# Unrolled attention pipeline: key products one tile early, new slots for every step, joined narrow maxima, expert weights loaded into the front's buffers

## The reference, cut to what matters

```python
x = x + layernorm(L0_attn(layernorm(x)))     # x: 8 x 1024 x 256
x = x + layernorm(L0_ffn(layernorm(x)))

# L0_attn, per position, 16 heads of 16:
Q, K, V = rms(x, g1) @ Wq.T, rms(x, g1) @ Wk.T, rms(x, g1) @ Wv.T
kv1[e,d] = sum_h elu(K)[h,e] * V[h,d] * SCALE     # e in the first half of a head, kv2: in the second
attn[h,d] = sum_e elu(Q)[h,e] * kv1[e,d] - lmb * (the same with kv2)
attn = rms(head norm(attn), g3) + head norm(attn)
out = gelu(attn @ W1) @ W2.T + attn

# L0_ffn: causal softmax attention (16 query heads, 4 key heads, rotary), then 8 experts, 2 per token:
h = clip(residual + softmax(q k^T / 4, causal) v @ Wo)
o = (silu(f @ Wg[e]) * (f @ Wu[e])) @ Wd[e]     # f = rmsnorm(h), for the two chosen e
out = clip(h + sum of the two, weighted)
```

## Time and profile before

| | |
|---|---|
| median of 3 runs | 4241.21 us (4240.19 to 4244.3) |
| profiled execution | 4237.51 us, its span 4235.6 us |
| busy in the span | PE 3146.7, DVE 2483.6, POOL 1651.6, ACT 1599.7 us |
| mean granted TensorE clock | 0.843 |
| front | to about 3304 us; experts' matmuls about 3350 to 4143 us; the rest is the last layer norm |

### The profile page before, as it was taken

The page is one execution under the profiler, slowest core; times in us unless marked ns, Lnnn a source line. Parts: engine busy times, 40 slices in busy tenths (PEclk is TensorE's granted clock), DMA queues, the critical chain, the costliest instruction groups (busy, mean ns, idle before and its releaser), DMA issues. The chain is left out here.

```text
span 4235.6 us, 54665 instructions
## 1 busy us (share of the span) xinstructions
PE 3146.7 (74%) x17668; PEld 1857.1 (44%) x17669; DVE 2483.6 (59%) x5036; ACT 1599.7 (38%) x3644; POOL 1651.6 (39%) x2045
## 2 busy tenths in 40 slices
PE   3555777777767776777777677767887399999991
PEld 2433434443443444444434444443433266666660
DVE  4667776776677667767776776676563122222225
ACT  1222445444534443443345444435544122222223
POOL 4564433543553354345435443541312122222222
PEclk7677888788888888887888888888888699999995
DMA  1000000000000000000000000000000533333335
GB/s 36 3 9 7 7 9 9 10 19 7 22 14 14 14 15 21 9 19 9 20 7 20 16 13 13 14 17 6 21 16 30 161 61 55 55 60 56 55 52 164
DMA packets 102336, 123.25 MB, mean 29 GB/s; under 512 B 14048, under 2 KB 89824, under 8 KB 102112
## 3 DMA queue, kind: packets, MB, share of 16 engines
q1 hardware_dynamic: 76384, 85.54, 6.7%
q0 software_dynamic: 25728, 34.88, 4.8%
HBM read 58.23 MB, written 61.36 MB: 28 GB/s over the span
## 5 line engine op out<-in xcount | busy, mean ns | idle before, releaser
L752 ACT ACTIVATE PR<-SP_ 128x512 f32<-128x512 f32 (+3 forms) x1536 | 728.0, 490 | 1528.6 <-PE SP_ L1366 1019.0
L1042 DVE TENSOR_REDUCE NM<-MX 128x1 f32<-128x512 f32 (+3 forms) x1536 | 817.1, 551 | 657.3 <-PE MX L1322 398.2
L1319 PE MATMUL MX<-KST,QST 96*128 96x512 bf16 (+3 forms) x1536 | 540.6, 362 | 407.3 <-DVE NM L1042 353.9
L472 POOL TENSOR_TENSOR P<-QK,VS 128x2048 f32<-128x2048 f32 x128 | 478.8, 3740 | 860.8 <-DVE QK L863 860.8
L1363 PE MATMUL SP_<-QST,KST 99*128 99x512 bf16 (+3 forms) x1536 | 544.0, 357 | 67.4 <-ACT PR L752 53.7
L1319 PEld LDWEIGHTS MX<-KST,QST 96*128 96x128 bf16 x1536 | 155.8, 102 | 770.5 <-DVE NM L1042 560.4
L1646 POOL DMA_INDIRECT scratch_h<-Y,XG x136 | 211.6, 1556 | 632.4 <-DVE Y L1709 538.8
L1214 PE MATMUL SUM<-ident,P 128*128 128x128 f32 x2048 | 313.0, 319 | 138.1 <-POOL P L472 83.5
L1687 DVE TENSOR_TENSOR AG<-UB,SL 128x512 f32<-128x512 f32 x136 | 94.0, 691 | 488.5 <-PE UB L1726 488.5
L1380 PE MATMUL OA<-PR,V 128*32 128x512 f32 (+3 forms) x3072 | 354.4, 536 | 0.8 <-ACT PR L752 0.6
L1214 PEld LDWEIGHTS SUM<-ident,P 128*128 128x128 f32 x2048 | 285.3, 168 | 158.3 <-issue 68.8
(11 more groups left out here) (245 smaller groups left out, 5399.1 us busy)
## 6 DMA issues: line engine op xcount, KB each, us to landing
XG<-scratch_xs SPq DMA_DIRECT2D x136, 130.0 KB, 2.1
X<-in_L_attn_x SPq DMA_DIRECT2D x64, 128.0 KB
scratch_x<-X SPq DMA_DIRECT2D x64, 128.0 KB, 1.8
scratch_h<-H SPq DMA_DIRECT2D x64, 128.0 KB, 1.7
X<-scratch_x SPq DMA_DIRECT2D x16, 512.0 KB, 4.0
HH<-scratch_h SPq DMA_DIRECT2D x16, 512.0 KB
out<-X SPq DMA_DIRECT2D x16, 512.0 KB, 3.2
wg<-in_L_ffn_Wg SPq DMA_DIRECT2D x1, 4096.0 KB, 13.9
```

The source lines that it names most:

```text
L472: sg["prod1"].by(pool.tensor_tensor(P1[:, half].rearrange("p (h e d) -> p h e d", h=hh, e=HD), QK[:, t % 2, D:2 * D][:, r].rearrange("p (h ...
L752: sg["exp"].by(act.activation(PR[:, n % 8, q0:512], SP_[:, n % 2, q0:512], ACT.Exp))
L1042: sg["mx"].by(dve.tensor_reduce(NM[:, u % 2, part, i, h:h + 1], MX[:, index % 2, 0:n], AX.X, ALU.max, negate=True))
L1319: m = pe.matmul(out, QST[0:MROW, j % 2, g * G + h, i * P:(i + 1) * P], KST[0:MROW, keys % RK, g, 0:n], start=True, stop=not last)
```

## The change

In words:

- The pipeline starts one period earlier (p = -2), and tile p + 1 is normalized, projected and put through `elu` inside period p. `key_products` are quarters (4 heads): three behind `elu(p + 1)` and the fourth behind `out_coefficients`. `sum_heads` of tile p stand in slots 0 and 2 of period p. `query_products` and `query_sums` are quarters too, with two buffers P2, in slots 3 to 19.
- `parts` is taken apart: its three copies go to ScalarE (`first_part`, `second_part`, `second_again`), its three sums stay on VectorE. `add_gains` and the clipping of H2 go to GpSimd.
- All other steps have new slots; `logits` goes from slot 5, behind the split, to slot 21, one slot after `route`.
- Maxima over narrow key ranges are joined: four heads of 128 keys, or two of 256, fill one bank, with one mask matmul and one reduction. The plan's lead times have new numbers, and TensorE waits for the reader itself of the ring's bank.
- The buffers of experts' weights are allocated for the whole program, and the front's buffers are views into them (`carve`). Wg and Wu are loaded in pieces in periods 72 to 75, Wd behind the last row of the front.

The core of the diff, key products and SyncE's weight loads first:

```diff
-                def key_products(t, half):
+                def key_products(t, k):
...
-                        need("heads_summed", 2 * t - 1 + half)
+                        need("heads_summed", 2 * t - 1 + k // 2)
...
+                def load_weight(w, name, experts):
+                    for e in experts:
+                        sp.dma_start(w[:, e], a["L0_ffn_" + name][e].rearrange("(c p) f -> p c f", p=P)).then_inc(wsem, 16)
...
+                        if p - TT in (8, 9, 10, 11) and i in (3, 15):
+                            n = 2 * (p - TT - 8) + (i == 15)
+                            if n == 0:
+                                front_done()
+                            load_weight((wg, wu)[n // 4], ("Wg", "Wu")[n // 4], range(2 * (n % 4), 2 * (n % 4) + 2))
...
+                need("lg", TT)
+                load_weight(wd, "Wd", range(E))
```

GpSimd's slots:

```diff
+                        if i == 10 and have(p + 1):
+                            key_products(p + 1, 0)
+                        if i == 12 and have(p + 1):
+                            key_products(p + 1, 1)
+                        if i == 12 and have(p + 1):
+                            key_products(p + 1, 2)
+                        if i == 14 and have(p - 17):
+                            clip(p - 17)
...
+                        if i == 19 and have(p - 6):
+                            out_coefficients(p - 6)
+                        if i == 19 and have(p + 1):
+                            key_products(p + 1, 3)
```

VectorE's slots:

```diff
-                        if i == 0 and have(p - 1):
-                            query_sums(p - 1, 1)
-                        if i == 1 and have(p - 8):
-                            parts(p - 8, 0)
-                        if i == 2 and have(p):
-                            elu(p)
...
-                        if i == 5 and have(p - 18):
-                            logits(p - 18)
...
-                        if i in (20, 22) and have(p):
-                            query_products(p, (i - 20) // 2)
-                        if i == 21 and have(p):
-                            query_sums(p, 0)
+                        if i == 3 and have(p):
+                            query_products(p, 0)
+                        if i == 5 and have(p - 8):
+                            third_part(p - 8)
+                        if i == 6 and have(p):
+                            query_sums(p, 0)
+                        if i == 6 and have(p - 1):
+                            norm_heads(p - 1)
+                        if i == 7 and have(p):
+                            query_products(p, 1)
+                        if i == 9 and have(p + 1):
+                            elu(p + 1)
+                        if i == 9 and have(p):
+                            query_products(p, 2)
```

TensorE's slots, and the joined pieces:

```diff
-                        if i == 8 and have(p):
-                            sum_heads(p, 0)
...
-                        if i == 16 and have(p):
-                            sum_heads(p, 1)
...
+                        if i == 0 and have(p):
+                            sum_heads(p, 0)
+                        if i == 2 and have(p):
+                            sum_heads(p, 1)
+                        if i == 4 and have(p):
+                            turn_sums(p)
...
+                    for k in range(heads):
+                        m = pe.matmul(out[:, k], QST[0:MROW, j % 2, g * G + h + k, i * P:(i + 1) * P], KST[0:MROW, keys % RK, g, 0:n],
+                                      start=k == 0, stop=not last, skip_group_check=True)
                     if last:
-                        m = pe.matmul(out[:, n - P:n], identb[:, :], mask_qk[:, :], start=False, stop=True)
+                        m = pe.matmul(out[:, :, n - P:n], identb[:, :], mask_qk[:, :].unsqueeze(1).broadcast_to([P, heads, P]),
+                                      start=False, stop=True, skip_group_check=True)
```

489 lines of the change are left out of this document (260 added, 229 removed).

## The result

The changed kernel took 3368.93 us (median of 4 runs, 3362.46 to 3372.2), the kernel before 4240.99 (4 runs). The ratio is 0.7941, with a 95% interval of 0.7927 to 0.7954. The prediction was 3763 us (3590 to 4010): the direction was right, the time came out 394 us lower.

What follows compares the result with a forecast made beforehand. The prediction took in-order programs waiting for one another, not one engine's work, to bound the kernel. Terms of -385 (52 periods), -65, +13, -12 and -29 made -478 us, giving 3763 us, range 3590 to 4010.

Steps and rivals of the forecast that it cites:

- The 29.8 us for LG go: Eight middle tiles: TensorE's 29.8 us wait for VectorE's logits vanishes, with L944 gone from between and second_layer well before logits.
- GpSimd's long product shuts out VectorE's copy: Split's cast L944: takes 3.67 us beside a GpSimd key half, against 0.33 for a cast of the same shape.
- VectorE 233 us: Eight middle tiles: VectorE's busy time goes from 275 to about 233 us.
- TensorE's busy time 267: Eight middle tiles: busy time falls from 288 to 267 us, 6 by joined maxima and 15 by a higher clock.
- Ring 28, the rest 22, new waits 15: 65 us: TensorE's waits in eight middle tiles: ring about halved to 28, ScalarE and others 25 to 22, new waits 15 us.
- Sum 332, 41.5 a tile: Eight middle tiles: 267 + 28 + 22 + 15 = 332 us, 7.4 less a tile; bounds 37.2 and 50.8.
- Early tiles 19.2: Tiles without causal attention: the loop from turn_sums around takes 19.2 us against 24.0, and bounds only these tiles.
- The stretch with causal attention alone: -12: The 383 us from 2860 to 3243: twelve units lose 0.8 us and a few round trips, -12 us.
- Weights -29, pieces 0: Between front and experts: earlier weight loads save 29 us; pieces in periods 72 to 75 cost 0, at worst 20.
- Rival 2: TensorE becomes the only bound and stays at 2.4 GHz: 36 us a tile, about 3475 us; 12 in 100.
- Rival 3: GpSimd's and VectorE's products shut each other out: 52.8 us a tile, about 4415 us, slower; 5 in 100.
- Rival 1: Stalls move and don't vanish, VectorE waiting for turn_sums: 45.0 us a tile, about 3970 us; 22 in 100.

Runs made afterwards that it cites:

- before: The kernel without the change, 4240.99 us (median of 4 runs).
- products earlier: Kernel without the change, with the second head sum, turn_sums and the query products and sums moved to earlier slots of their own period: ratio 1.0446.
- maxima joined: Kernel without the change, with only the narrow maxima joined as in the change: ratio 0.9893.
- less query work: Kernel without the change, with query products and sums over only 2 of 8 heads in each half, other values constants: ratio 0.9365.
- after: The changed kernel, 3368.93 us (median of 4 runs), ratio 0.7941 to the kernel without the change.
- one lump: Changed kernel, overlap kept, with the eight quarters of query products and sums together in slot 9: ratio 0.9027.
- no overlap: Changed kernel, with project, exponentials, values, elu and all key quarters of the next tile behind this tile's last query sum: ratio 0.8719.
- both: Changed kernel with the edits of "no overlap" and "one lump" together: ratio 0.9535.
- not joined: Changed kernel without the joining of narrow maxima: ratio 0.8132.

## Why the prediction was wrong

**The cause, as far as shown.** Two things are shown by runs: many waits between the in-order engines went at once, and the granted clock rose with it. How the gain divides among the new slots is argued in part.

*The ring.* TensorE can issue two maxima ahead of VectorE, no more, and the old order had VectorE's long work close together: four query instructions of 2.3 us with a maximum or two between them, then the split with the 3.67 us cast. In the 48.3 us of ring waits VectorE's trace has it 15.8 in query products and sums, 14.7 in the cast L944 and 13.6 in maxima themselves; the four longest of these waits (4.2 to 6.4 us) all lie at the cast. To see how far the rule of the ring alone goes, I took for each use of the ring in the eight tiles the busy time of either engine since the use before, from the trace, and added them up with two rules only: a piece waits for the reduction two uses back, and a reduction waits for its piece. That gives the time TensorE would wait, had the ring been the only tie between them:

```
                 eight tiles  TensorE  VectorE  ring wait    ring wait
                 us           busy     busy     by the rule  in the trace
before           391.2        288.2    275.3    46.0         48.3
 products earlier 425.2       303.2    276.7    57.6         50.6
 maxima joined   385.7        279.8    273.8    39.4         32.6
 less query work 362.5        279.0    225.8    19.9         27.7
after            275.4        250.9    235.6    17.3         11.7
 one lump        341.3        263.1    243.2    68.7         65.7
 no overlap      320.9        266.9    260.2    27.0         22.9
 both            372.0        274.3    263.8    69.1         67.5
 not joined      284.1        252.6    239.8    25.7         19.8
```

The estimate follows the trace within 8 us in these nine kernels, though in the changed one that is half again too much (17.3 and 11.7). The ring wait thus depends strongly on where VectorE's work stands against TensorE's: with one lump VectorE has 7.6 us more busy time than in "after" and TensorE waits 54.0 us more. It depends on how much there is, too: with less query work it fell from 48.3 to 27.7. Why "products earlier" was slower is argued alone: the query work got into slots where TensorE has less else to do than in slots 20 to 2, and no run tests it by itself.

*The other ties.* The larger part of the idle time that went lies where engines wait for each other once a tile outside the ring: LG, `elu`'s inputs, the sums. In "before" idle time beyond the ring was 103.0 - 48.3 = 54.7 us, after 24.5 - 11.7 = 12.8. The overlap takes some of these ties off the path (without it, 54.0 - 22.9 = 31.1 us again), and `logits` a slot behind `route` with `second_layer` ahead of both takes off another 2.0 us a tile.

*The clock.* In the eight tiles of "before" TensorE's clock was at its lower level for 133.1 us, and TensorE was busy in 86.3 of them; in "after" it was there for 10.2 us, busy throughout. If the same work takes half as long at the upper level, an estimate from these two, it saves 38 us; TensorE's busy time fell by 37.3. The kernel with maxima not joined says the same: its 1832 matmuls take 252.6 us, and in "before" 288.2.

*What the sum of the parts is.* What single edits undone in the changed kernel cost, in us: overlap 330, the place of `route` 123, halves for quarters 96, joining 81, the plan's numbers 53, weights 28, casts 20. Their sum is 731 of the 872. The other 141 us are the remaining new slots and what the parts do together, and no run divides them. The lump's 461 us don't belong in this sum, since the old order had no unbroken block.

**My steps, one by one.**

- *What bounds it: no engine, the waits of in-order programs.* Right. What I read off the waits was wrong: I treated 48.3 (ring), 29.8 (LG) and 25 as separate items with a price each. Three runs say otherwise: edits that took 16 to 28 us out of one wait gave 10 to 17 to others (casts, joined maxima, `second_layer`).
- *The 29.8 us for LG go, since L944 no longer stands between.* The wait went, but this reason was wrong: without the cast in the old order it grew to 39.4. The other reason that I gave, `second_layer` well before `logits`, was the right one: with `second_layer` behind `route` again it is back at 12.4 us.
- *GpSimd's long product shuts out VectorE's copy.* It holds as a duration; as a price it was small: 20 us in all in the old order, and as much in the new one, where the casts stand beside no key product.
- *VectorE 233 us.* 235.6. *Quarters at most 0.1 us more each:* 1212 ns for half of 2284, 0.07 us.
- *TensorE's busy time 267 (bounds 261 and 288 less 6).* **Failed:** 250.9. I took 15 us for the clock, 27 at most; it rose from 0.83 to 0.98, and that was worth some 36 (288.2 - 252.6, the same 1832 matmuls without joining). The trace of "before" could have told: half of the 86.3 us busy at the lower level is 43, by the same estimate. Joining, for which I took 6, gave 1.7 (252.6 to 250.9). The lower bound was a slip as well: 288 less 6 less 27 is 255 and not 261, which would have made 292 us of the lower 298, still too high.
- *Ring 28, the rest 22, new waits 15: 65 us.* **Failed, the largest step:** 24.5 in all. The ring was 11.7 and not 28, all else 12.8 and not 37. I left the rest nearly as it was without a reason, and added new waits: without overlap it is 31.1, so the overlap alone takes 18.3 of it, and the new wait of VectorE for SUM is only 5.9. The ring's wait I halved by the length of the longest instruction (2.3 to 1.2 us). Halves in the changed kernel cost 7.9 us of it in eight tiles. How long VectorE works without a maximum between counts for more: eight instructions of 1.2 us in a row cost 54.0.
- *Sum 332, 41.5 a tile.* 275.4, 34.4 a tile. The 56.6 us are 16 of busy time and 40.5 of waits. Between tiles 12 and 63 the periods lost 715.9 us and not 385: 331 of the 394 us.
- *Early tiles 19.2.* 20.3. To tile 12, -74.7 against -52.
- *The stretch with causal attention alone: -12.* **Failed in size:** about -47 (75.5 less 28.9): 383 us at 0.88 became 340 at 0.94 with nearly as many matmuls. TensorE's busy time fell from 322.1 to 301.8, which is the clock again, and its idle time from 60.9 to 38.2.
- *Weights -29, pieces 0.* 28.9 by the trace, 28 by the run. Right, both.
- *Rival 2 (TensorE the only bound, at 2.4 GHz, 12 in 100)* is nearest to what happened, down to the 91 per cent. It gave 36 a tile from 261 us of work; the work was 250.9, and its 3475 us are still 106 too many. The nearest row, 2860 to 3243, had 84 per cent busy at a clock of 0.88; the range's lower end should have taken this rival in.
- *Rival 3 (products shut each other out)* fell. All 256 product quarters of the trace took at most 1.22 us, 82 of them partly beside a key quarter and 3 wholly; the key quarters took 1.94 at most. *Rival 1* did not occur: VectorE waits 5.9 us for SUM in eight tiles, 0.7 a tile, where 3 would have decided for it.

## What to carry to other kernels

- Where two in-order engines meet through a ring of two buffers, look at how evenly their work alternates, and not at their totals alone. Walk both programs from one use of the ring to the next, and add up the excess of either side. Eight unchanged instructions in a row instead of spread out cost 461 us of 3369 here.
- Waits of one lagging engine are not a list of items: cure one and the next in order grows. Price a wait by what remains if its engine is as late as before; in this case the rewrite that changed all at once gained far more than the single edits that ran in the old order (casts, joined maxima and the place of `second_layer` alone brought 20, 45 and 54 us, the whole 872).
- Idle time of TensorE costs twice: the same 1792 matmuls, but for a few, took 250.9 us with 24.5 us of idle time among them, 263.1 with 78.2 and 266.9 with 54.0. TensorE was busy at the lower level for 10.2, 45.8 and 39.8 us of these; that the third has more busy time than the second is not explained by this. Let the clock into the estimate at its upper level when the idle time goes.

## What the runs showed of the hardware

- TensorE's granted clock was 0.98 over 1699 us of mixed work at 91 per cent busy, and 0.96 to 0.99 in the eight tiles of every kernel with no idle piece over 3.2 us there. It was 0.93 without overlap, with two pieces over 5 us in eight tiles, and 0.79 to 0.87 in the kernels with four or more. The worst is "products earlier": 303.2 us for the 1832 matmuls that took 288.2 before.
- VectorE's `norm_heads` L975, with both inputs in SBUF, takes 0.41 us in an early tile and 669 ns on average in the late ones, where it often stands beside GpSimd's rotations L571 and L572. `add_residual` L996, again with both inputs in SBUF, took 0.42 us in the 47 tiles in which no key quarter stood beside it, and 1.14 on average, 1.50 at most, in the 17 others. The cast L1058 of 4 elements a row took 0.16 us by itself and 1.83 just behind the start of a key quarter. Products with one operand in PSUM, reductions from SBUF (36 of them wholly inside a key quarter, 1.21 us at most) and maxima from PSUM (215 inside, 0.69 at most) were not slowed. It is what the Trainium skill ("SBUF — State Buffer", section "SBUF: two separate sides") says of two-input operations, and the trace agrees.
